# The head of a one-core AdaLN-FFN kernel in another order: GpSimd shares the parameter arithmetic, small loads move, four banks turn x, and the first Toeplitz tile is loaded in two column halves

## The reference

```
K[h, l] = 2 * Re( sum_n C[h,n] * (exp(dtA[h,n]) - 1) / A[h,n] * exp(dtA[h,n] * l) )     h < 64, n < 64, l < 1024
y       = mask * ( causal_conv(mask * x, K) + D * mask * x )
out     = x + ( (y @ Wg) * sigmoid(y @ Wg) * (y @ Wu) ) @ Wd        Wg, Wu: 1024 x 2752, Wd: 2752 x 1024
```

## Time and profile before

| what | value |
|---|---|
| median of 3 runs | 1187.47 us (1185.72 to 1187.68) |
| the profiled execution | 1186.11 us, its span 1184.3 us |
| TensorE busy | 1155.2 us (98% of the span) |
| VectorE busy | 891.4 us (75%) |
| ScalarE busy | 848.6 us (72%) |
| GpSimd busy | 221.0 us (19%) |
| mean granted TensorE clock | 0.992 |

### The profile page before, as it was taken

One profiled execution on the slowest core, in us unless ns is written; L12 is line 12 of the kernel. 1 busy time (PEld: TensorE's weight loads), 2 busy tenths in 40 slices (PEclk: granted clock), 3 DMA queues, 4 the chain that ended last, 5 costly groups with the idle time before them and its releaser, 6 DMA issues.

```text
span 1184.3 us, 15015 instructions
## 1 busy us (share of the span) xinstructions
PE 1155.2 (98%) x5562; PEld 952.6 (80%) x5562; DVE 891.4 (75%) x964; ACT 848.6 (72%) x1396; POOL 221.0 (19%) x136
## 2 busy tenths in 40 slices
PE   5899999999999999999999999999999999999996
PEld 4899998788788878878878878888888888888883
DVE  6698854777777777777777898887777777777775
ACT  6533212888788788788878797778788788788773
POOL 0022000211332332121121241211211211211213
PEclk9899999999999999999999999999999999999999
DMA  8587868531464366434443775555434434444514
GB/s 296 159 267 247 286 200 266 145 81 54 116 162 114 108 163 158 130 100 107 107 107 95 239 206 153 163 177 143 107 103 111 107 103 111 107 101 113 151 48 166
DMA packets 66975, 173.94 MB, mean 147 GB/s; under 512 B 11654, under 2 KB 17222, under 8 KB 66902
## 3 DMA queue, kind: packets, MB, share of 16 engines
q1 hardware_dynamic: 66870, 172.95, 50.8%
q0 software_dynamic: 32, 0.03, 0.0%
HBM read 159.94 MB, written 15.83 MB: 148 GB/s over the span
## 4 chain that ended last, share of the span: by engine, by line
PE 92%; SPq 3%; DVE 2%; DMA 1%; issue 1%; POOL 0%; ACT 0%; DVEq 0%; POOLq 0%
PE pair L1211 27%; PE pair L1232 26%; PE pair L1252 26%; PE pair L1166 10%; DMA toep<-kernel_padded 1%; SPq L352 1%; DMA kernel_padded<-k_sb 0%; PE pair L1146 0%; POOL o L591 0%; DVE arg L746 0%; DVE y_nat L881 0%; PE pair L1281 0%; PE pair L1314 0%; SPq L377 0%; DVE turns L841 0%
## 5 line engine op out<-in xcount | busy, mean ns | idle before, releaser
L985 DVE SCALAR_TENSOR_TENSOR acc<-pair,s_down,acc 128x1024 f32<-128x1024 f32 x328 | 420.5, 1283 | 197.8 <-PE pair L1252 197.4
L667 ACT ACTIVATE pair<-pair,ratio 128x512 f32<-128x512 f32 x616 | 381.7, 665 | 100.5 <-PE pair L1211 100.2
L686 ACT ACTIVATE pair<-pair,ratio 128x512 f32<-128x512 f32 x581 | 360.2, 659 | 122.0 <-PE pair L1232 121.9
L1211 PE MATMUL pair<-high,wg 128*128 128x512 f32 x704 | 278.8, 396 | 0.0
L1211 PE MATMUL pair<-low,wg 128*128 128x512 f32 x704 | 276.5, 393 | 0.0
L1232 PE MATMUL pair<-high,wu 128*128 128x512 f32 x672 | 267.7, 398 | 0.4 <-DVE sil L963 0.4
L1252 PE MATMUL pair<-mid_h,wd 128*128 128x512 f32 x688 | 267.7, 391 | 0.0
L1252 PE MATMUL pair<-mid_l,wd 128*128 128x512 f32 x672 | 264.7, 394 | 0.0
L1232 PE MATMUL pair<-low,wu 128*128 128x512 f32 x672 | 263.2, 392 | 0.0
L543 POOL CAST mid_h<-sil 128x1024 fp32r<-128x1024 f32 (+1 forms) x43 | 45.1, 1049 | 695.7 <-DVE sil L963 685.0
L1211 PEld LDWEIGHTS pair<-high,wg 128*128 128x128 f32 x704 | 132.1, 188 | 31.7 <-ACT pair L667 1.1
(11 more groups left out here) (157 smaller groups left out, 598.8 us busy)
## 6 DMA issues: line engine op xcount, KB each, us to landing
q_in<-rows_backwards SPq DMA_DIRECT2D x86, 512.0 KB, 4.6
z_in<-zeros_plus_one SPq DMA_DIRECT2D x130, 256.0 KB, 4.7
toep<-kernel_padded SPq DMA_DIRECT2D x64, 512.0 KB, 6.7
q_in<-_L_ffn_down_qweight_dram SPq DMA_DIRECT2D x42, 512.0 KB, 4.8
u_all<-in_x_dram SPq DMA_DIRECT2D x16, 512.0 KB, 10.0
x_fin<-in_x_dram SPq DMA_DIRECT2D x12, 512.0 KB, 8.3
out_dram<-x_fin SPq DMA_DIRECT2D x12, 512.0 KB, 5.3
high_parts<-staged SPq DMA_DIRECT2D x8, 512.0 KB, 3.0
```

What stands on the lines that cost most here:

```text
L667: act.activation(gate_ps[:, tb, :], gate_ps[:, tb, :], ACT.Copy, scale=ratio[:, 0, G * t + g:G * t + g + 1]).then_inc(gate_scaled, 1)
L686: act.activation(up_ps(tau)[:, tb, :], up_ps(tau)[:, tb, :], ACT.Copy, scale=ratio[:, 1, G * t + g:G * t + g + 1]).then_inc(up_scaled, 1)
L985: dve.scalar_tensor_tensor(out=acc[:, hid, :], in0=ps, scalar=scale, in1=acc[:, hid, :], op0=ALU.mult, op1=ALU.add).then_inc(down_taken, 1)
L1211: mm = pe.matmul(gate_ps[:, tb, :], w["g"][tau % 2][:, g, :], rows[:, g, 512 * tb:512 * tb + 512], start=g == 0 and part == 0, stop=part = ...
```

## The change

- `log_dt`, `ident` and x groups 0 to 2 are issued by ScalarE's DMA queue at the start. SP issues `log_A`, `A_imag`, `C`, the table, then x groups 3 to 11.
- `shifts` and `load_rows` leave the place ahead of `store_kernels(0)` and go into SP's loop at g = 1, ahead of `load_toeplitz(3)`. x groups 12 and 13 go behind `load_toeplitz(0)`, 14 and 15 behind `load_toeplitz(1)`.
- The first channel's Toeplitz tile is loaded in two DMAs: columns 512 to 1023 first (semaphore `first_columns`), then columns 0 to 511. TensorE's first four diagonals wait for the first, the others for the second.
- GpSimd computes the polynomial of exp(dtA) - 1, the norm of A, the product of C with the conjugate of A (`w_re`, `w_im`) and four of the eight copies into `par_h`. VectorE keeps the sine and cosine arguments, the reciprocal and the last products.
- Exp of chunks 0 and 1 is one activation over eight channels (`exp_sizes(0, 0, 8)`). Chunks now have places of their own in the buffers (`place_of`), so the angles of a chunk needn't wait for the chunk before.
- Turns use four banks for groups 0 to 11 (`HEAD_TURNS = 12`), and so wait for the copy four halves back. Turns 12 to 15 stand behind convolution groups 0 to 3. `multiply_kernel(1)` goes ahead of the first convolution.
- The order on VectorE and ScalarE changes: the mask is made behind `reduce_angles(1)`, `ident16` is cast at g = 4.

The diff, cut to its core:

```diff
@@ SP
-            sp.dma_start(logs[:, 0:1], log_dt.rearrange("(h o) -> h o", o=1)).then_inc(logs_in, 16)
             sp.dma_start(logs[:, 1:1 + NS], log_A).then_inc(logs_in, 16)
             sp.dma_start(ai_in[:], A_imag).then_inc(ai_loaded, 16)
+            sp.dma_start(c_in[:], C).then_inc(c_loaded, 16)
             sp.dma_start(tab[:], ctab).then_inc(tab_in, 16)
...
-            for g in range(3, NG):
+            for g in range(6, HEAD_TURNS):
                 sp.dma_start(x_in(g), x_rows(g)).then_inc(x_loaded[g], 16)
...
+                    at, left = (g * HG + hh) * KPAD, L
+                    if g == 0 and hh == 0:
+                        left = L // 2
+                        sp.dma_start(toep[:, slot, left:L], bass.AP(kpad.tensor, at + left, [[1, P], [1, L - left]])
+                                     ).then_inc(first_columns, 16)
+                    sp.dma_start(toep[:, slot, 0:left], bass.AP(kpad.tensor, at, [[1, P], [1, left]])
+                                 ).then_inc(t_loaded[slot], 16)
...
-            sp.dma_start(shifts[:], stab).then_inc(shifts_in, 16)
-            load_rows()
             store_kernels(0)
             load_toeplitz(0)
+            for g in range(HEAD_TURNS, HEAD_TURNS + 2):
+                sp.dma_start(x_in(g), x_rows(g)).then_inc(x_loaded[g], 16)
             store_kernels(1)
             load_toeplitz(1)
+            for g in range(HEAD_TURNS + 2, NG):
+                sp.dma_start(x_in(g), x_rows(g)).then_inc(x_loaded[g], 16)
...
                 if g == 0:
                     store_kernels(2)
+                if g == 1:
+                    sp.dma_start(shifts[:], stab).then_inc(shifts_in, 16)
+                    load_rows()
@@ GpSimd (new)
+            do(both(norm[:], ai_in[:], ai_in[:], ALU.mult), both(w_re[:], ci, ai_in[:], ALU.mult),
+               both(w_im[:], cr, ai_in[:], ALU.mult))
+            pool.wait_ge(are_ready, 1)
+            do(pool.tensor_scalar(near_0[:], are[:], -0.25, 0.25, ALU.max, ALU.min),
+               both(v1, eA, eA, ALU.mult))
+            do(pool.tensor_scalar(near[:], near_0[:], 1 / 5040.0, 1 / 720.0, ALU.mult, ALU.add),
+               both(v2, cr, eA, ALU.mult))
+            both(norm[:], norm[:], v1, ALU.add).then_inc(norm_ready, 1)
+            for c in (1 / 120.0, 1 / 24.0, 1 / 6.0, 0.5, 1.0):
+                do(both(near[:], near[:], near_0[:], ALU.mult))
+                do(pool.tensor_scalar(near[:], near[:], c, None, ALU.add))
+            do(both(near[:], near[:], near_0[:], ALU.mult))
+            do(pool.tensor_scalar(near_0[:], are[:], -0.25, None, ALU.is_ge))
+            pool.wait_ge(first_done, 1)
+            do(both(near[:], near[:], near_0[:], ALU.mult),
+               pool.tensor_scalar(far, exp_are[:], 1.0, None, ALU.subtract),
+               pool.tensor_scalar(near_0[:], near_0[:], -1.0, 1.0, ALU.mult, ALU.add))
+            do(both(far, far, near_0[:], ALU.mult))
+            both(em1[:], near[:], far, ALU.add).then_inc(em_ready, 1)
+            do(both(v1, ci, eA, ALU.mult), both(w_re[:], w_re[:], v2, ALU.subtract))
+            do(both(w_im[:], w_im[:], v1, ALU.add))
+            pool.wait_ge(inv_ready, 1)
+            both(w_re[:], w_re[:], inv[:], ALU.mult).then_inc(w_ready, 1)
+            both(w_im[:], w_im[:], inv[:], ALU.mult).then_inc(w_ready, 1)
+            pool.wait_ge(aim_ready, 1)
+            for n in range(2):
+                pool.tensor_copy(par_h[:, 0, n, :], are[:]).then_inc(par_ready, 1)
+                pool.tensor_copy(par_h[:, 1, n, :], aim[:]).then_inc(par_ready, 1)
@@ ScalarE (new order)
+            act.dma_start(logs[:, 0:1], log_dt.rearrange("(h o) -> h o", o=1)).then_inc(logs_in, 16)
+            act.dma_start(ident[:], ident_in).then_inc(ident_in_sb, 16)
+            for g in range(3):
+                act.dma_start(x_in(g), x_rows(g)).then_inc(x_loaded[g], 16)
...
+            take_rows(0, 4)
+            sizes(1, 0, 8)
+            act.activation(warm[:], ident[:, 0:1], ACT.Sin)
+            take_turned(4, 0)
+            angles(0)
+            take_turned(4, 1)
+            take_rows(5, 10)
+            angles(1)
+            take_rows(10, HEAD_TURNS)
+            sizes(2, *place_of(2))
+            angles(2)
@@ VectorE (order)
+            exp_sizes(0, 0, 8)
+            turn_angles(0)
+            reduce_angles(0)
...
+            combine(0)
+            turn_angles(1)
+            dve.wait_ge(d_loaded, 16)
+            take_kernel(0)
+            reduce_angles(1)
             for c in range(KT):
                 dve.tensor_scalar(mask_t[:, c, :], lens[:], col(C_LCOL + c), None, ALU.is_gt)
...
             combine(1)
+            exp_sizes(8, 8, 8)
+            turn_angles(2)
             take_kernel(1)
@@ TensorE
-            for g in range(6):
+            for g in range(3):
                 turn(g)
             pe.wait_ge(par_ready, 8)
...
-            for g in range(6, 10):
+            for g in range(3, 7):
                 turn(g)
...
-                    if g < 2 and hh == 1:
-                        multiply_kernel(1 + g)
+                    if g == 1 and hh == 1:
+                        multiply_kernel(2)
...
             multiply_kernel(0)
-            for g in range(10, 13):
+            for g in range(7, HEAD_TURNS):
                 turn(g)
+            multiply_kernel(1)
             for hc in range(NG // 4):
                 for q in range(4):
                     convolve(hc, q)
-                    if 4 * hc + q < 3:
-                        turn(13 + q)
+                    if HEAD_TURNS + 4 * hc + q < NG:
+                        turn(HEAD_TURNS + 4 * hc + q)
```

More of the change, by code:

```diff
@@ L810, in _ @@
-            dve.wait_ge(c_loaded, 16)
-            cr, ci = c_in[:, :, 0], c_in[:, :, 1]
-            do(times(t1[:], cr, zr[:]), times(t2[:], ci, zi[:]), times(t3[:], cr, zi[:]), times(em1[:], ci, zr[:]))
-            do(dve.tensor_tensor(t1[:], t1[:], t2[:], ALU.subtract), dve.tensor_tensor(t3[:], t3[:], em1[:], ALU.add))
-            for n in range(2):
-                dve.tensor_copy(par_h[:, 0, n, :], are[:]).then_inc(par_ready, 1)
-                dve.tensor_copy(par_h[:, 1, n, :], aim[:]).then_inc(par_ready, 1)
-                dve.tensor_scalar(par_h[:, 2, n, :], t1[:], 2.0 - 4.0 * n, None, ALU.mult).then_inc(par_ready, 1)
-                dve.tensor_scalar(par_h[:, 3, n, :], t3[:], 2.0 - 4.0 * n, None, ALU.mult).then_inc(par_ready, 1)
+            dve.wait_ge(w_ready, 2)
@@ L1144, in multiply_kernel @@
                     pe.wait_ge(k_sb_ready, c)
-                for h in range(CHUNKS[c][1]):
-                    mm = pe.matmul(k_ps[0:32, 32 * h:32 * h + 32], left[:, h, :], right[:, h, :],
+                at, n = place_of(c)
+                for h in range(n):
+                    mm = pe.matmul(k_ps[0:32, 32 * h:32 * h + 32], left[:, at + h, :], right[:, at + h, :],
                                    start=True, stop=True)
@@ L1165, in convolve @@
                     for d in range(KT):
+                        if n == 0 and d == KT // 2:
+                            pe.wait_ge(t_loaded[slot], 16)
                         mm = pe.matmul(
```

253 lines of the change are left out of this document (125 added, 128 removed).

## The result

The changed kernel took 1197.41 us, the median of four runs (1196.34 to 1199.42); the kernel before took 1186.60 beside it (four runs, 1184.70 to 1187.68). The ratio is 1.0095 with an interval of 1.0074 to 1.0116: about 11 us slower. The forecast was 1192.9, with a range up to 1197.0. The direction and the place were right; the size was not, and the time lies just above the range. The profiled execution took 1196.54 with a span of 1194.7, against 1184.3 before, so 10.4 us are to be found between the two traces. The end is the same in both kernels: 10.1 us idle in the last 34.7 of the changed one.

What follows compares the result with a forecast made beforehand. TensorE was taken as the bound (92% of the chain). Group 3 2.15 late, slow channel 2.4 and fourth turn 0.9 gave about +5.4 on the profiled 1186.1: 1191.5, or 1192.9 on the median's scale; range 1185.5 to 1197.

Steps and rivals of the forecast that it cites:

- SP's list holds TensorE ahead of group 3: Main case: 17 moved DMAs ahead of `load_toeplitz(3)` make TensorE wait, +2.4 to +7.5 us; chance 0.60.
- chunk 2's k_sb comes at 48.2, 6.75 us earlier: Chunk 2's finished kernel piece, 14.2 us after the first convolution's start, at 48.2 instead of 54.95.
- T0: Start of the first convolution on TensorE: 34.0 us forecast, bounds 33.2 to 36, against 37.79 before.
- GpSimd's chain: Parameter arithmetic in the head: 0.26 us an operation, 0.08 a wait, `em_ready` at 13.8, `par_ready` full at 16.4.
- Both waiting and 0.75 of VectorE go: From k_sb to the second combination's end: Exp already done, so 2.45 of table waiting and 0.75 vanish; 5.8 us remain.
- The slow first channel: TensorE starts group 3 slowly after its gap: 2.4 us more for the first channel.
- The fourth turn: One more turn within the convolutions, now behind group 3: 0.9 us more on TensorE at the fast level.
- SP's 17 DMAs: Issue of `shifts` and 16 row DMAs on SP ahead of `load_toeplitz(3)`: 13.0 us, bounds 7 and 14.8.
- rival A: The head pays and SP doesn't hold it; 17 issues at 0.46, start 8.5 earlier, 1184.6 us, faster; chance 0.12.
- SP is behind TensorE's new times from there on, and adds nothing: From group 4 on, SP's loads cause no further delay beyond the +5.4 us.
- B: Rival: GpSimd is the bound, `par_ready` 3 us later or more, start only 3.75 earlier, +8.4, 1195.9 us; chance 0.12.
- C: Rival: rows take 10 us on SP, start 8 earlier, +1.2, 1188.7 us, nothing measurable; chance 0.16.

Runs made afterwards that it cites:

- the one of the best parts: Changed kernel with rows and x groups issued early, group 14's Toeplitz loads ahead of the first weight loads, parameters on VectorE: 1181.79 us, ratio 0.9955.

## Why the prediction was right in direction and too small

**The sum's mechanism held.** "SP's list holds TensorE ahead of group 3" is what the trace and three of the kernels show: with the rows moved alone most of the loss is there, with them back in the head it is gone, with other loads in their place a wait is back.

**The step that failed is the earlier start: "chunk 2's k_sb comes at 48.2, 6.75 us earlier".** It came at 52.20, 2.75 earlier. From the first convolution on, the step was right (14.2 forecast, 52.20 - 37.65 = 14.55 measured). Nearly all of the error, 3.65 of 4.0, is in T0, 37.65 instead of 34.0 and past the upper bound of 36. It has two parts.

- GpSimd's chain. 0.26 an operation, by a line through two large subtractions, was too low: those with two inputs took 0.28 to 0.31 (once 0.40), and of the ten with one input eight took 0.36 to 0.44. The prediction had taken 0.2 off for one-input operations; most of them were the dearer ones. `par_ready` was full at 19.0, not 16.4, which the prediction had named as a sign against itself ("only after 18"). From the end of `are` to the end of `em` an operation took, with its gaps, (15.88 - 7.04) / 22 = 0.40, where the forecast had 7.1 / 22 = 0.32. The bounds held this (12.5 to 22). What failed is the choice of the value: a line through two shapes was carried down to an eighth of the smaller one. With the parameters back on VectorE they were ready 2.36 earlier, and the first convolution started 1.68 earlier.
- The second combination. From k_sb to its end 7.5 us passed (29.71 to 37.22), 5.8 were forecast. "Both waiting and 0.75 of VectorE go" was wrong: VectorE still waited 1.85 for ScalarE's `turns`. ScalarE had the copies of turns 7 to 11 to make, and those turns ran at the lower clock level and took 7.32. The changed kernel's chain of waits runs through them: 24 transposes from 29.11 to 34.46, a copy, ScalarE's `turns` and the combination. With rows and x early the granted clock was 0.69 and 0.74 over 28 to 31 and 31 to 34, the turns took 6.25, and from k_sb to the end of the second combination 6.73 passed (29.72 to 36.45). This part is read from the traces; no experiment changed the clock there alone.

By the trace, 2.7 of the 3.65 us are there when `par` is copied (19.78 against 17.1), 3.0 at k_sb (29.71 against 26.7) and 4.7 at the second combination's end (37.22 against 32.5); the forecast had set T0 0.8 above the bound of 33.2, which takes the rest back.

**The other terms, one by one.** The wait ahead of group 3: about 9 forecast, 7.43 measured. The slow first channel: 2.4 and 2.2 (11.50 - 9.28 for the four channels together). The fourth turn: 0.9 and 0.91. The landing: 4.0 and 4.2. SP's 17 DMAs: 13.0 and 10.2, so the rows had indeed been stretched by the queue they stood in, and rival A's reason was half true. The head shows it too: behind x groups up to 11 the 17 took 10.6 (10.51 to 21.11), behind all x groups 14.2 (13.31 to 27.54). Against that stood a term that the sum did not have: 1.9 for chunk 2's store, which lands behind the x groups 14 and 15. The prediction let them cost only their issue time, hidden. Had the first convolution started at 34.0, all this would give 8.50 - 3.65 = +4.9 at group 4, where +5.4 was forecast: two errors of about 2 to 3 us each cancelled, which is luck, and the head's did not.

**"SP is behind TensorE's new times from there on, and adds nothing"** was nearly right: 0.92 ahead of group 8 and 0.17 at group 14.

**The rivals.** B came nearest: GpSimd later by 2.6 where B says 3 or more, and +8.50 measured at group 4 where it says +8.4. That the numbers meet is in part luck: 0.40 an operation with its gap is short of B's 0.5, and the second combination, which B does not name, added another 1.7. B had 0.12, by the row nearest to it too little: no row of before showed a small GpSimd operation, and the term that the whole head stood on deserved a wider spread. A did not: 10.2 of issue against 2.75 earlier. C's combination did not come.

**The pages.** ScalarE's load at 22.29 follows a copy that ends at 22.27 and takes 1.28, so this trace too has no drain of 1.38 as the Trainium skill ("ScalarE: Activation LUTs", What ACT_TABLE_LOAD costs) states it; leaving it out was right. The contention of the shared port (the Trainium skill, "GPSIMD Engine Reference", Key points) does show: beside GpSimd VectorE's `SCALAR_TENSOR_TENSOR` of 64x64 took 0.18 to 0.35, three of them 0.34 or 0.35; where GpSimd was idle it was 0.21 or 0.22. The prediction held that VectorE would only wait shorter for `em_ready`. That is right for its chain; but the six series steps ahead of `are` took 1.69, while GpSimd made its first products from 4.81. With the parameters on VectorE they took 1.49, and so they did in the kernel with the rows early, where GpSimd began only at 6.65. The 0.2 that the earlier loads had brought (first operation at 3.21, 3.41 before) was lost there before `are` began, and the 0.4 us of the forecast came to nothing.

**GpSimd's cost is its own.** From 11.39 to 15.99 VectorE is idle in the changed kernel, and GpSimd's operations there take 0.31 with two inputs and 0.36 or 0.37 with one (one of them 0.24), and a step of the series 0.84 or 0.85, against 0.86 beside VectorE. So contention is not what made the chain long.

**Still open.** How the 3 us between the medians with rows early (1187.20) and with x early as well (1184.13) come about: the two traces differ by 0.8 at the end of the convolutions, and the profiled execution of the latter, 1186.21, was the slowest of its ten.

## What to carry to other kernels

A load that nobody needs soon still costs its issue time on the queue that brings the next tile: before moving a list of DMAs behind a loop's start, subtract the slack of each later tile (issue plus landing against use) from the list's length, and add the slow start of TensorE behind the gap that it makes. Moving a chain of small dependent operations to an idle engine lengthens it if each operation is dearer there or a step needs more of them; a chain that decides the head belongs on the engine with the shortest small operation, even if that one is the busier. And a gain at the head has to be followed to the end: here the Toeplitz loads that stood behind weight loads took back 3 us of it.

## What the runs showed of the hardware that was not expected

- On GpSimd most small one-input operations were dearer than those with two inputs. In the changed kernel, at 64x64 f32: `TENSOR_SCALAR` mostly 0.36 to 0.38, once 0.44, and 0.24 and 0.29 in the two that multiply and add in one; `TENSOR_TENSOR` 0.28 to 0.31, once 0.40. On VectorE they were 0.18 and 0.21.
- A store of one kernel piece lands in 1.4 to 1.5 us on quiet queues. It took 3.4 to 5.7 behind Toeplitz loads with 1 MB of x, and 3.8 and 6.4 (the kernel with rows and x early, and the one of the best parts) behind Toeplitz loads alone.
- The issue time of a DMA on SP did not go by its bytes: 0.32 for a row of 256 bytes, 0.33 for a store, 0.43 for a Toeplitz tile of 512 KB; for the moved rows 0.59 to 0.62 for the 128-partition rows of scales and 0.75 to 0.82 for those of line 397 and 408. One form is not fixed either: the row of 256 bytes took 0.49 to 0.60 in the head, and a row load up to 2.50 behind the x groups.
